# Attention kernel: PSUM banks dealt three to scores and three to maxima, with one exponential per bank

## The reference

```python
for lvl in range(LEVELS):
    stride = 2 ** lvl
    x = query[:, ::stride, :]
    outs.append(_mha(x, in_proj_w[lvl], in_proj_b[lvl], out_w[lvl], out_b[lvl]))
...
scores = jnp.einsum('bhqd,bhkd->bhqk', q, k) / jnp.sqrt(jnp.asarray(hd, x.dtype))
attn = jax.nn.softmax(scores, axis=-1)
out = jnp.einsum('bhqk,bhkd->bhqd', attn, v)
...
x = _layernorm(x + _L0_attn_ref(x, ...), axis=-1)
x = _layernorm(x + _L0_ffn_ref(x, ...), axis=-1)
```

## Time and profile before

| | us |
|---|---|
| median of 3 runs | 4471.17 (4460.4 to 4474.56) |
| profiled execution | 4468.91 |
| its span in the profile | 4467.1 |
| PE busy | 3904.1 (87%) |
| DVE busy | 2665.8 (60%) |
| ACT busy | 2448.1 (55%) |
| POOL busy | 1160.8 (26%) |
| granted clock of PE, mean | 0.943 |

### The profile page before, as it was taken

The page is one execution under the profiler, slowest core; times in us unless marked ns, Lnnn a source line. Parts: engine busy times, 40 slices in busy tenths (PEclk is TensorE's granted clock), DMA queues, the critical chain, the costliest instruction groups (busy, mean ns, idle before and its releaser), DMA issues. The chain is left out here.

```text
span 4467.1 us, 69697 instructions
## 1 busy us (share of the span) xinstructions
PE 3904.1 (87%) x20881; PEld 2152.1 (48%) x20881; DVE 2665.8 (60%) x4841; ACT 2448.1 (55%) x3163; POOL 1160.8 (26%) x1000
## 2 busy tenths in 40 slices
PE   4599989989989988998998998963999999999998
PEld 2233333333333333333333333323887877877787
DVE  2287777777777777777777777836333333333333
ACT  1376756756756756665675675643444444434343
POOL 4334433424423433433443342220000000000000
PEclk7799999999999999999998999976999999999999
DMA  5443343334344344343334334115000000000000
GB/s 179 101 84 85 97 83 91 92 84 92 91 77 90 101 84 84 101 86 78 84 96 85 91 91 79 29 55 208 10 11 11 20 11 11 20 11 11 10 20 10
DMA packets 308843, 307.47 MB, mean 69 GB/s; under 512 B 75168, under 2 KB 285280, under 8 KB 308192
## 3 DMA queue, kind: packets, MB, share of 16 engines
q1 hardware_dynamic: 299200, 293.59, 26.7%
q10 hardware_dynamic: 9216, 8.39, 0.5%
HBM read 202.28 MB, written 96.47 MB: 67 GB/s over the span
## 5 line engine op out<-in xcount | busy, mean ns | idle before, releaser
L736 ACT ACTIVATE a_probs<-a_p_s 128x1024 f32<-128x1024 f32 x1360 | 1323.1, 1021 | 734.2 <-PE a_p_s L992 725.5
L810 DVE TENSOR_REDUCE a_part_max<-a_p_m 128x1 f32<-128x512 f32 x2048 | 1337.9, 680 | 436.7 <-PE a_p_m L1007 431.9
L1007 PE MATMUL a_p_m<-a_k_st,a_q_st 96*128 96x512 bf16 (+2 forms) x2944 | 1024.5, 380 | 252.2 <-DVE a_part_max L810 153.7
L1387 PE MATMUL p_h<-f_h_hi,f_w_hi 128*128 128x512 f32 x2048 | 811.4, 396 | 40.0 <-issue 35.4
L992 PE MATMUL a_p_s<-a_q_st,a_k_st 98*128 98x512 bf16 (+2 forms) x2944 | 830.7, 370 | 17.6 <-ACT a_probs L736 12.0
L1007 PEld LDWEIGHTS a_p_m<-a_k_st,a_q_st 96*128 96x128 bf16 x2944 | 260.9, 98 | 1174.9 <-DVE a_part_max L810 779.1
L1387 PE MATMUL p_h<-f_h_lo,f_w_hi 128*128 128x512 f32 x2048 | 807.2, 394 | 1.9 <-issue 1.9
L1024 PE MATMUL a_p_o<-a_probs,a_v_aug 128*17 128x512 f32 (+2 forms) x5888 | 740.6, 583 | 0.8 <-ACT a_probs L736 0.8
L1356 DVE TENSOR_TENSOR f_h_lo<-f_h_f,f_h_hi 128x512 fp32r<-128x512 f32 x256 | 177.2, 692 | 721.8 <-ACT f_h_hi L1269 721.8
L810 DVE TENSOR_REDUCE a_row_max<-a_p_m 128x1 f32<-128x512 f32 (+2 forms) x672 | 440.3, 680 | 187.3 <-PE a_p_m L1007 182.1
L1267 ACT ACTIVATE f_h_f<-p_h,f_sc 128x512 f32<-128x512 f32 x256 | 176.6, 690 | 582.5 <-PE p_h L1387 582.5
(11 more groups left out here) (113 smaller groups left out, 4584.8 us busy)
## 6 DMA issues: line engine op xcount, KB each, us to landing
qk_scratch<-a_qk_bf SPq DMA_DIRECT2D x96, 384.0 KB, 2.4
a_w_lo<-wqkv_inner SPq DMA_DIRECT2D x32, 768.0 KB, 4.3
a_q_st<-qk_scratch SPq DMA_DIRECT2D x192, 128.0 KB, 6.1
a_k_st<-qk_scratch SPq DMA_DIRECT2D x192, 128.0 KB, 6.4
a_q_st<-qk_scratch SPq DMA_DIRECT2D x336, 64.0 KB, 2.6
a_k_st<-qk_scratch SPq DMA_DIRECT2D x336, 64.0 KB, 2.6
a_a_lo<-a_attn SPq DMA_DIRECT2D x384, 32.0 KB, 2.0
a_o_lo<-wo_inner SPq DMA_DIRECT2D x24, 512.0 KB, 3.5
```

The source lines that it names most:

```text
L736: act.activation(probs[:, s % 2, 2 * p:2 * p + 2, :], p_s[:, 2 * p:2 * p + 2, :], ACT.Exp, scale=HD ** -0.5).then_inc(exp_done.sem, 1)
L810: dve.reduce_max(out, src, AX.X).then_inc(max_read.sem, 1)
L1007: ins = pe.matmul(p_m[:, n % 2, r * size:(r + 1) * size], q_st[0:ROWS, unit.place, j, q * 128:(q + 1) * 128], k_st[0:ROWS, unit.halves[kb] ...
L1387: ins = pe.matmul(out, a, c, start=first and n == 0, stop=last and n == len(terms) - 1)
```

## The change

`p_s` gets three banks and `p_m` three. A score task is now one head and one bank, and so is its exponential: 2720 exponentials of 512 columns in place of 1360 of 1024. The banks are used in turn, 0, 1, 2. Since 340 tasks per batch are no multiple of three, the last one takes bank 1, and `BANK_FREED[n]` says how many earlier tasks must be done for the bank of task n: n - 2 nearly everywhere (task n - 3 is done), n - 1 for n = 1 and n = 339. `exp_done` and `score_mm` count single heads, and `max_read` counts in steps of two. The places in `timeline` change from .4 and .7 to .4, .41, .7 and .71.

```diff
+BANK_OF = [n % 3 for n in range(4 * STEPS - 1)] + [1]
+BANK_FREED = [max(m + 1 for m in range(-4, n) if BANK_OF[m] == BANK_OF[n]) for n in range(4 * STEPS)]
...
-        p += [(s + .4, "score", 2 * s), (s + .7, "score", 2 * s + 1), (s + (2.1 if s < STEPS - 1 else 1.3), "value", s)]
+        p += [(s + (.4, .41, .7, .71)[j], "score", HG * s + j) for j in range(HG)] + [(s + (2.1 if s < STEPS - 1 else 1.3), "value", s)]
...
-        p_s = pb("p_s", [128, 4, 512])
-        p_m = pb("p_m", [128, 2, 512])
+        p_s = pb("p_s", [128, 3, 512])
+        p_m = pb("p_m", [128, 3, 512])
...
-                            s, p = divmod(n, 2)
+                            s, j = divmod(n, HG)
                             act.wait_ge(score_mm.sem, score_mm.value(it, n + 1))
                             value_mm.wait(act, it, s - 1 if s else 0)
-                            act.activation(probs[:, s % 2, 2 * p:2 * p + 2, :], p_s[:, 2 * p:2 * p + 2, :], ACT.Exp,
-                                           scale=HD ** -0.5).then_inc(exp_done.sem, 1)
+                            act.activation(probs[:, s % 2, j, :], p_s[:, BANK_OF[n], :], ACT.Exp, scale=HD ** -0.5).then_inc(exp_done.sem, 1)
...
-                            exp_done.wait(pe, it, n - 1)
-                            for j in (2 * p, 2 * p + 1):
-                                for i in range(parts):
-                                    half, key = divmod(i * size + kt * 128, W)
-                                    ins = pe.matmul(p_s[:, j, i * size:(i + 1) * size], k_st[0:ROWS + 2, unit.halves[half], j, key:key + 128],
-                                                    q_st[0:ROWS + 2, unit.place, j, i * size:(i + 1) * size], start=True, stop=True)
+                            exp_done.wait(pe, it, BANK_FREED[n])
+                            for i in range(parts):
+                                half, key = divmod(i * size + kt * 128, W)
+                                ins = pe.matmul(p_s[:, BANK_OF[n], i * size:(i + 1) * size], k_st[0:ROWS + 2, unit.halves[half], j, key:key + 128],
+                                                q_st[0:ROWS + 2, unit.place, j, i * size:(i + 1) * size], start=True, stop=True)
...
-                            max_read.wait(pe, it, n - 1)
+                            max_read.wait(pe, it, BANK_FREED[n])
...
-                            pe.wait_ge(exp_done.sem, exp_done.value(it, 2 * n + 2))
+                            pe.wait_ge(exp_done.sem, exp_done.value(it, HG * n + HG))
```

More of the change, by code:

```diff
@@ L525, in steps @@
                                     hold()
-                            score_mm.wait(sp, it, 2 * freed_at(us))
+                            score_mm.wait(sp, it, HG * freed_at(us))
                             hold()
@@ L808, in steps @@
                                 out = slot[:, m * parts:(m + 1) * parts]
-                            src = p_m[:, n % 2, :].rearrange("p (r t) -> p r t", r=parts) if parts > 1 else p_m[:, n % 2, :]
-                            dve.reduce_max(out, src, AX.X).then_inc(max_read.sem, 1)
+                            src = p_m[:, BANK_OF[n], :].rearrange("p (r t) -> p r t", r=parts) if parts > 1 else p_m[:, BANK_OF[n], :]
+                            dve.reduce_max(out, src, AX.X).then_inc(max_read.sem, 2)
                             if lvl == 0 and m == 4 * UNITS[u].tiles - 1:
@@ L985, in steps @@
                             size = W // parts
-                            if kt == 0 and p == 0:
+                            if kt == 0 and j == 0:
                                 neg_placed[u % 2].wait(pe, it, u // 2 + 1)
-                            exp_done.wait(pe, it, n - 1)
-                            for j in (2 * p, 2 * p + 1):
-                                for i in range(parts):
-                                    half, key = divmod(i * size + kt * 128, W)
-                                    ins = pe.matmul(p_s[:, j, i * size:(i + 1) * size], k_st[0:ROWS + 2, unit.halves[half], j, key:key + 128],
-                                                    q_st[0:ROWS + 2, unit.place, j, i * size:(i + 1) * size], start=True, stop=True)
+                            exp_done.wait(pe, it, BANK_FREED[n])
[3 more added lines that the diff above has]
+                                                q_st[0:ROWS + 2, unit.place, j, i * size:(i + 1) * size], start=True, stop=True)
                             ins.then_inc(score_mm.sem, 1)
@@ L1006, in steps @@
                                 key = q * 128 // size * size if parts > 1 else 0
-                                ins = pe.matmul(p_m[:, n % 2, r * size:(r + 1) * size], q_st[0:ROWS, unit.place, j, q * 128:(q + 1) * 128],
+                                ins = pe.matmul(p_m[:, BANK_OF[n], r * size:(r + 1) * size], q_st[0:ROWS, unit.place, j, q * 128:(q + 1) * 128],
                                                 k_st[0:ROWS, unit.halves[kb], j, key:key + size], start=True, stop=True)
```

4 lines of the change are left out of this document (2 added, 2 removed).

## The result

The changed kernel takes 4518.92 us (median of four runs, 4513.32 to 4520.97), beside 4472.86 us for the kernel before (four runs, 4460.4 to 4476.26). The ratio is 1.0106, with a 95% interval from 1.0084 to 1.0128: slower by 46 us. The profiled execution took 4519.83 us, 1.8 of it outside its span.

What follows compares the result with a forecast made beforehand. The prediction took plain attention steps as bound by the loop through two max banks, projection and neg steps by PE. Its terms, 159 - 139 - 38 - 20 + 70 + 4 = 36, gave 4505 us, range 4405 to 4595.

Steps and rivals of the forecast that it cites:

- (a): Scores in three banks: s3 waits for the exponential of s0, 0.25 us late per step; +159 us, bounds 76 and 223.
- (b): Maxima in three banks: m1 waits for m2's reduction, not m3's, shortening plain steps; 139 us less, bounds 100 and 160.
- (c): Places where DVE is late for long: one more bank lets m1 and the value go ahead; 38 us less.
- (d): PE's granted clock: fewer slow returns at 1.2 GHz after waits; 20 us less, bounds 0 and 40.
- Rival 3: PE's mean granted clock in the attention falls from 0.95 to 0.90: 4656 us; chance 0.04.
- (e): Late exponentials on ACT lose their cover, s3 waits for them at once; +70 us, bounds 45 and 110.
- (f): Added ACT exponentials: 216 us more busy time, hidden in its waits; +4 us at the batches' edges.
- Rival 2: ACT becomes the pace setter, with single exponentials of 0.69 us and costlier late ones: 4609 us; chance 0.14.

Runs made afterwards that it cites:

- run 1: The changed kernel with the maxima back in two banks, scores still in three: 4580.41 us, ratio 1.0263 to the kernel before.
- run 11: The changed kernel with s3 behind the next step's m0 and m1, and the maxima in two banks: 4566.55 us, ratio 1.0216.
- run 4: The changed kernel with PE's order value, s0, m0, s1, m1, s2, m2, s3, m3, then other work: 4469.39 us, ratio 1.0005.
- run 7: run 4 with POOL's sum tasks .7 of a step later, behind a_rstd: 4424.95 us, ratio 0.9902.
- run 8: run 2 with POOL's sum tasks .7 of a step later: 4403.83 us, ratio 0.9859.
- run 10: The changed kernel with s3 behind the next step's m0 and m1, and POOL's sum tasks .7 of a step later: 4393.83 us, ratio 0.9822.
- run 6: The changed kernel with ACT's projection copies at .57 of a step instead of .3, the opening excepted: 4514.58 us, ratio 1.012.
- run 2: The kernel before with one exponential per bank, keeping four score banks and two max banks: 4440.99 us, ratio 0.9948.
- run 5: The changed kernel with only s3 moved, behind the next step's m0 and m1 and ahead of the value product: 4442.15 us, ratio 0.9943.
- run 3: The changed kernel with exponentials covering 256 of 512 columns, the other probabilities held constant: 4424.13 us, ratio 0.9899.
- run 9: The kernel before once more, with nothing changed, one execution: 4469.63 us.
- run 12: The kernel before with 170 semaphore increments that nobody waits for added to PE's program behind its attention: 4446.86 us, ratio 0.9961.

## Why the prediction was right, and where its sum was off

The prediction said 4505 us, slower by 36, in a range of 4405 to 4595; it is 4519. Direction and mechanism held in the attention; that nothing else would change did not.

- **(a), s3's wait.** Forecast: 1.12 after s0, 0.25 late. Measured: 1.15 in the usual step, 0.28 late, with ACT starting 0.50 after s0 and 602 ns, near what was taken from the earlier trace rows. Projection steps went up by 0.28 to 0.31 and neg steps by 0.28, to slightly more than the forecast 4.45 to 4.5 and 3.5; these are the steps where nothing hid it. The trace prices the term. The time from s0 to s3, added up over the 680 steps and less 0.87 each, is 35 us before and 301 in the changed kernel. Of these 266 us more, some 181 are the usual lateness (140 in the 535 steps where s3 is up to 1.2 after s0, and 0.28 in each of the other 145). The sum had 159, so 22 short.
- **(b), the third max bank.** Forecast: plain steps 3.13 to 3.09 and those with transposes to about 3.1. Measured: 3.04 to 3.12, and 183 of 302 are now under 3.2 where 122 were. PE's waits for `a_part_max` under 1 us went from 162 with 71 us to 36 with 13. (b), (c) and (d) together had been put at 197. The attention grew by 75 us with s3's part of the steps 266 longer, so the rest of it became 191 shorter: near the forecast. Taking the bank away gives other figures, 61 us in run 1, where s3's delay and the wait for the reductions lie side by side, and 124 in run 11, where s3 stands in the loop. So the terms hold for this change and add up only in its order.
- **(c), the long waits for DVE.** Forecast -38. PE's waits for reductions of at least 1 us went from 30 with 91 us to 21 with 61: -30, so 8 short. The longest was 7.4 and is 6.7: the bank lets PE go ahead a little, but what sets the time there is POOL's sum ahead of `a_rstd` (runs 4, 7, 8 and 10).
- **(d), the clock.** Forecast -20. Score products of 512 columns that show 0.5 us or more, as at the lower clock, went from 77 to 58 of 2560, which is the direction; its worth was not isolated. The prediction's "only behind waits near 2 us" was too narrow: the clock also fell behind waits of 1.59 us in the kernel before (at 856.91 the score pair shows 1.03 us for 0.60). Rival 3, a lower clock, did not come: 0.96 over the whole attention in both. The Trainium skill's rule on depth-cycling ("TensorE: Matmul & The Clock Gate", section "A second HAM failure mode: psum-queue depth-cycling") does not describe this kernel: s3 is 0.28 late in most steps and the clock stays up; it falls behind the waits of 3.2 us.
- **(e), late exponentials.** Forecast: +70, waits for `a_probs` of 100 us or more. Measured: the other 85 of the 266 us under (a), with the 4 of the edges in them, so 11 short. The wait rows say 106.8 us in 112 waits, 94 more than before, 14 of them over 3 us (45 us). The prediction had one place 3.1 us late in each batch; the trace before has two in each of the first seven. And it was not ACT's order to mend: with the copies later the time turned up in front of the projections (run 6).
- **(f), the split.** Forecast: hidden. Run 2 shows it: 2803.6 us of attention for 2809.1. Rival 2 had no ground.

So the attention rose by 75 us where the sum had 36: s3's part was 266 for 233, the rest -191 for -197. Undoing s3's place gave 77 us and not 266. In run 5 s3 stands in the loop of the max banks, and runs 3, 4 and 7 suggest that part of what each step saves is waited away at the batch's edge and behind POOL's chain: steps with a projection are most often 4.24 again, but their mean is 5.15 where it was 4.93 before the change. How much each of the two takes is not separated. The error that no step of the prediction could have held is the other one: "the change touches nothing there, so the whole effect lies in the attention". The feed-forward part gave 25 us back, and without that the profiled execution would have been 4545. That the total came out 14 us from the forecast is luck to that extent; the direction and the range would have held without it.

## What to carry to other kernels

When banks are dealt anew, count in the producer's own order how much time lies between filling a bank and filling it again, and compare it with start delay + consumer + release (here 0.50 + 0.60 + 0.04 us against 0.87); a shortage is paid in every step in which the producer is otherwise busy. It can be cured without a bank, by moving one product behind work that is ready: one place in the order gave 77 us with three max banks. It gave only 14 with two, since the new place lay in the other ring's loop, so look at both loops before moving. And a bank moved from one ring to the other is worth what both rings make of it: with the order mended on either side, three and three banks (run 10) and four and two (run 8) end within 10 us. Saved step time is kept only if no fixed chain waits further on, so look at the long waits before adding up the short ones: putting POOL's sum behind `a_rstd` gave 37 to 48 us in three versions.

## What was not expected of the hardware

The feed-forward part's loop takes 1504.0 us behind the attention in one program and 1479.0 or 1481.3 in another with the same instructions there. In the program before, PE stops in this loop at 3439.03 for 4.42 us, at 3525.94 for 2.68, and so on, nine times, mostly twice a pass; in the changed one once a pass, five times (the wait rows count 11 and 6, with short ones ahead of the loop). The profile names nothing that PE waited for ("issue"). Behind each such stop the matmuls run at the lower clock for a while:

```profile
3439.03 0.79 PE L1387 MATMUL p_h<-f_h_hi,f_w_hi 128*128 128x512 f32 x1 [4.42 <-issue]
3439.61 0.63 PE L1387 MATMUL p_h<-f_h_lo,f_w_hi 128*128 128x512 f32 x1
3440.04 0.63 PE L1387 MATMUL p_h<-f_h_hi,f_w_hi 128*128 128x512 f32 x1
```

The profile's list of DMA queues has one for instructions. For 3434 to 3440 us, around this stop, it is the only queue listed:

```profile
q8 instruction: 3, 0.05, 4.5%
```

That is three packets of 16 KB, two of them within the stop and one behind it. In each of the nine stops before and the five after, one or two such packets start between 0.2 us before and 1.0 us behind the moment at which PE falls idle, two in the stops of 4.2 us and more, one in those of 2.5 to 3.2, and PE goes on 1.3 to 2.3 us after the last has landed. Packets of this queue also come between the stops, without a stop. So PE stops while a block of its instructions is fetched, as far as times can show it.

The stops themselves make 13 of the 25 us (37.3 to 24.2). Their number repeats in a second execution of the same program (run 9, 37.1 us in 11) and changes when 170 idle instructions are put ahead of the loop (run 12: five stops in the loop, as in the changed kernel). So what decides is the program's length ahead of the loop, or where the loop's code lies; how the placement acts on it stays open. The Trainium skill ("Runtime: NRT & Kernel Launch", section "Instruction fetch mechanics") says that an engine is fed its instructions in blocks in sequence, and that a taken branch to a place outside the blocks at hand makes it stop for a fetch. The packets in the stops, which repeat with the passes, agree with this; which branch it is no row here shows. For a comparison of two kernels it means that some 0.5% can come from a part that neither change touched, and that the two parts' spans are worth reading apart.
